# Keys and values of a second batch moved into the last head of the first, output weighting moved to ScalarE and accumulating transfers

## The reference, cut to what matters

```
xn = layernorm(x)
x  = x + attention(xn) + experts14(xn)      # 8 causal heads of 128, one key/value head; each row to 1 of 14 experts
xn = layernorm(x)
x  = x + scan(xn) + experts8(xn)            # selective state scan, 16 states; each row to 2 of 8 experts
```

## Time and profile before

| | |
|---|---|
| median of three runs | 759.58 us |
| profiled execution, its own time | 764.21 us |
| its span in the trace | 762.4 us |
| TensorE matmul busy | 672.0 us (88%) |
| VectorE busy | 539.8 us (71%) |
| ScalarE busy | 410.7 us (54%) |
| GpSimd busy | 236.7 us (31%) |
| mean granted TensorE clock | 0.951 of full |

### The profile page before, as it was taken

The page is one execution under the profiler, slowest core; times in us unless marked ns, Lnnn a source line. Parts: engine busy times, 40 slices in busy tenths (PEclk is TensorE's granted clock), DMA queues, the critical chain, the costliest instruction groups (busy, mean ns, idle before and its releaser), DMA issues. The chain is left out here.

```text
span 762.4 us, 11200 instructions
## 1 busy us (share of the span) xinstructions
PE 672.0 (88%) x3434; PEld 467.7 (61%) x3446; DVE 539.8 (71%) x830; ACT 410.7 (54%) x825; POOL 236.7 (31%) x183
## 2 busy tenths in 40 slices
PE   3988999999998989888899999998679779888685
PEld 2856777677765984544566566565535779878332
DVE  6165444344422224439899999999999999999998
ACT  1145665555651545575766667665746556666220
POOL 0012202212200005100222432332012866788874
PEclk9999999999997899999999999999969899999688
DMA  8400000000055482012366867778782454554112
GB/s 294 156 4 12 8 8 7 14 10 8 8 170 166 140 294 56 18 36 89 91 149 165 202 177 195 180 176 211 196 212 72 139 171 125 160 162 119 31 44 81
DMA packets 59806, 86.79 MB, mean 114 GB/s; under 512 B 7505, under 2 KB 35922, under 8 KB 59762
## 3 DMA queue, kind: packets, MB, share of 16 engines
q1 hardware_dynamic: 41330, 57.89, 24.6%
q0 software_dynamic: 7680, 23.08, 14.1%
q10 hardware_dynamic: 10752, 5.24, 2.3%
HBM read 54.60 MB, written 14.81 MB: 91 GB/s over the span
## 5 line engine op out<-in xcount | busy, mean ns | idle before, releaser
L1578 DVE TENSOR_REDUCE nmax<-PS 128x1 f32<-128x128 f32 (+7 forms) x128 | 96.1, 751 | 109.0 <-PE PS L1015 108.7
L1043 PE MATMUL PS<-ROOM 128*128 128x512 f32 (+3 forms) x384 | 141.7, 488 | 0.7 <-ACT ROOM L682 0.7
L682 ACT COPY ROOM<-PS 128x512 f32<-128x512 f32 (+1 forms) x192 | 85.8, 483 | 91.9 <-PE PS L1027 91.0
L689 ACT ACTIVATE ROOM<-PS,nmax 128x128 f32<-128x128 f32 (+7 forms) x128 | 95.6, 747 | 47.7 <-DVE nmax L1578 45.6
L1027 PE MATMUL PS<-CST,ROOM 128*128 128x128 f32 x576 | 85.9, 277 | 7.0 <-ACT ROOM L682 7.0
L559 POOL DMA_DIRECT2D ROOM<-ROOM x32 | 28.4, 889 | 202.0 <-DVE ROOM L1662 202.0
L1027 PEld LDWEIGHTS PS<-CST,ROOM 128*128 128x128 f32 x576 | 64.6, 142 | 34.3 <-issue 24.5
L1043 PEld LDWEIGHTS PS<-ROOM 128*128 128x128 f32 x384 | 65.0, 191 | 29.8 <-issue 25.8
L1012 PE MATMUL PS<-LATER 128*128 128x512 f32 (+2 forms) x192 | 74.5, 498 | 7.0 <-ACT ROOM L689 3.9
L524 POOL DMA_INDIRECT rows_in<-XN,slot x48 | 66.6, 1388 | 27.7 <-DVE slot L1491 14.4
L1654 DVE TENSOR_TENSOR_SCAN ROOM<-ROOM 128x1024 f32<-128x1024 f32 x32 | 72.8, 2275 | 0.9 <-ACT ROOM L725 0.2
(11 more groups left out here) (178 smaller groups left out, 1238.3 us busy)
## 6 DMA issues: line engine op xcount, KB each, us to landing
ROOM<-bc_rows SPq DMA_DIRECT2D x32, 512.0 KB, 4.3
ROOM<-ROOM POOLq DMA_DIRECT2D x32, 512.0 KB, 6.2
LATER<-in_w SPq DMA_DIRECT2D x48, 256.0 KB, 2.8
ROOM<-in_w SPq DMA_DIRECT2D x32, 321.0 KB, 3.8
rows_in<-zero SPq DMA_DIRECT2D x20, 256.0 KB, 3.3
LATER<-rows_in SPq DMA_DIRECT2D x24, 128.0 KB, 2.5
rows_out<-ROOM ACTq DMA_DIRECT2D x24, 128.0 KB, 2.2
ROOM<-rows_in SPq DMA_DIRECT2D x8, 256.0 KB, 4.2
```

The costliest lines, as they stand in the source:

```text
L682: nc.scalar.copy(dst, src).then_inc(s_ed, 1)
L689: nc.scalar.activation(PR[:, s, 0:nk], sc[:, 0:nk], ACT.Exp, bias=nmax[:, i % 4:i % 4 + 1], accum_out=rsum[:, i:i + 1]).then_inc(s_ex, 1)
L1043: r = mm(PS[:, 6, lo:BANK], V[:, j, :], PT[:, 4 * group + j, lo:BANK], start=j == 0, stop=True, skip_group_check=True)
L1578: nc.vector.tensor_reduce(nmax[:, i % 4:i % 4 + 1], sc[:, 0:(i + 1) * P], AX_X, ALU.max, negate=True).then_inc(s_nm, 1)
```

## The change

It has these parts.

1. TensorE's `keys_values(1)` is split into `keys(1)`, issued in `head_end` of head 7 between its last `turn` and its last `out_part`s, and `values(1)`, issued after these and ahead of the two projections. Their PSUM banks change to 0, 1 (keys) and 2, 3 (values). VectorE does its part of the keys between `inverse(7, 1)` and the two `add_out`. Before the experts TensorE now waits until the keys have left PSUM, and the first hidden product waits for the values' copies.
2. In batch 1 the identity product of the query becomes two fp32r products, of the identity with a high part PEH and with a low part PEL of pe. ScalarE makes PEH (one copy of 128x1024) ahead of the experts, after all scatters of the first expert layer; VectorE makes PEL (one subtraction) inside the experts. VectorE also copies the identity once at the start.
3. For heads 9 to 14 the weighting of the projection leaves VectorE. ScalarE's `weigh_out` writes bank 7 times the inverse row sum into a buffer OW (four instructions for each half), at tiles i = 3 and 7 of the next head, and GpSimd's `x_add` adds the half to x with an accumulating transfer. The additions of heads 8 and 15 stay on VectorE; head 15's wait for the transfers.
4. `combine_first(1)` moves from behind head 15 to the end of head 9.

```diff
@@ GpSimd
+            def x_add(g, s):
+                pool.wait_ge(s_we, 2 * g + 1 + s)
+                if g >= FIRST:
+                    pool.wait_ge(s_xo[s], 16 * (g - FIRST + 1))
+                else:
+                    pool.wait_ge(s_gu, NT)
+                nc.gpsimd.dma_start(X[:, TB + 4 * s:TB + 4 * s + 4, :], OW[:, 4 * s:4 * s + 4, :], accum_op=ALU.add
+                                    ).then_inc(s_xo[s], 16)
...
                     y_add(n, 1)
+                    x_add(FIRST + h - 1, 0)
...
                     y_add(n + 1, 1)
+                    x_add(FIRST + h - 1, 1)
@@ ScalarE
+            def weigh_out(g, s):
+                act.wait_ge(s_wo, 2 * g + 1 + s)
+                act.wait_ge(s_ri, 2 * g + 1 + s)
+                if g >= FIRST:
+                    act.wait_ge(s_xo[s], 16 * (g - FIRST + 1))
+                for t in range(4):
+                    r = nc.scalar.activation(OW[:, 4 * s + t, :], PS[:, 7, t * P:(t + 1) * P], ACT.Copy,
+                                             scale=rinv[:, 4 * s + t:4 * s + t + 1])
+                r.then_inc(s_we, 1)
...
+                    if pending and not split and i in (3, 7):
+                        weigh_out(g - 1, i // 4)
...
             keys_values(1)
+            act.wait_ge(s_sc[0], 16 * NT)
+            nc.scalar.copy(PEH[:], peT).then_inc(s_peh, 1)
@@ TensorE
                 if b:
-                    r = mm(bank(7), ident, peT[:, hf * BANK:(hf + 1) * BANK], start=False, stop=True)
+                    if isinstance(g, int) and g == HEADS:
+                        pe.wait_ge(s_pel, 1)
+                    mm(bank(7), identr[:], PEH[:, hf * BANK:(hf + 1) * BANK], start=False, stop=False)
+                    r = mm(bank(7), identr[:], PEL[:, hf * BANK:(hf + 1) * BANK], start=False, stop=True)
...
                 turn(g, 7)
+                if turned:
+                    turned()
                 for part in range(4):
                     out_part(g, b, 1, part)
...
-                head_end(g, b, 7)
+                head_end(g, b, 7, *((None, None) if b else (lambda: values(1), lambda: keys(1))))
...
-            keys_values(1)
+            pe.wait_ge(s_kf, 6)
             experts_first()
@@ VectorE
-                    if i == 3 and pending:
+                    if i == 3 and pending and not batch[0]:
                         add_out(g - 1, 0, x_prev)
...
-                    7: (lambda: first_drive(0, 0),)})
+                    7: (lambda: first_drive(0, 0), lambda: combine_first(1))})
...
-                head_end(7)
+                head_end(7, lambda: keys_values(1))
...
             dve.wait_ge(s_we, 32)
-            combine_first(1)
```

More of the change, by code:

```diff
@@ L84, in sem @@
             return ctx.enter_context(nc.semaphore(name))
+        with ExitStack() as second_half_of_XN:
+            second_half_of_XN.enter_context(nc.sbuf_tensor("under_PEH", [P, 3 * T], F32))
+            PEH = second_half_of_XN.enter_context(nc.sbuf_tensor("PEH", [P, T], F32R))
         X = sb("X", [P, NT, D])
@@ L136, in build @@
         HEAD_END, MOE_END, END = 53 * KB, 90 * KB, 133 * KB
+        identr = sb("identr", [P, P], F32R)
+        with ExitStack() as first_split:
+            PEL = first_split.enter_context(nc.sbuf_tensor("PEL", [P, T], F32R))
+            first_split.enter_context(nc.sbuf_tensor("under_KH", [P, END - T], F32))
+            KH, KL, QH, QL = (first_split.enter_context(nc.sbuf_tensor(n, [P, T], F32R)) for n in ("KH", "KL", "QH", "QL"))
         ROOM = sb("ROOM", [P, END])
-        with ExitStack() as first_split:
-            KH, KL, QH, QL = (first_split.enter_context(nc.sbuf_tensor(n, [P, T], F32R)) for n in ("KH", "KL", "QH", "QL"))
         LATER = sb("LATER", [P, 4 * T])
@@ L261, in build @@
         s_we = sem("projected_added")
+        s_xo = [sem(f"weighted_output_added{s}") for s in range(2)]
+        s_peh = sem("positions_high_ready")
+        s_pel = sem("positions_low_ready")
         s_mw = [sem(f"expert_weights{i}") for i in range(4)]
@@ L961, in _, with keys, values @@
             pe.wait_ge(s_cst, 16)
-            def keys_values(b):
-                quads = (2 * b, 2 * b + 1)
+            def keys(b):
                 pe.wait_ge(s_xnt, 2 * b + 2)
-                for q in quads:
+                for q in (2 * b, 2 * b + 1):
                     mm(bank(KEY_BANK[q]), wkv[:, 0:D], XNT[:, q * BANK:(q + 1) * BANK], start=True, stop=True).then_inc(s_kp, 1)
-                for q in quads:
-                    if q == 3:
-                        pe.wait_ge(s_kf, 5)
+            def values(b):
+                for q in (2 * b, 2 * b + 1):
                     for t in range(4):
@@ L978, in _ @@
             pe.wait_ge(s_cnv, 1)
-            keys_values(0)
+            keys(0)
+            values(0)
             transposes(1)
@@ L1108, in head, with head_end @@
                         out_part(g, b, 0, i - 6, not opening)
-            def head_end(g, b, h, between=None):
+            def head_end(g, b, h, between=None, turned=None):
                 turn(g, 6)
@@ L1535, in _ @@
             cp(identb[:], ident)
+            cp(identr[:], ident)
             cp(causalb[:], cst["causal"])
@@ L1561, in keys_values, with positions_low @@
                     tt(KL[:, sl], QF, KH[:, sl].bitcast(F32), ALU.subtract).then_inc(s_ke, 1)
+            def positions_low():
+                dve.wait_ge(s_peh, 1)
+                tt(PEL[:], peT, PEH[:].bitcast(F32), ALU.subtract).then_inc(s_pel, 1)
             keys_values(0)
@@ L1592, in add_out @@
                     dve.wait_ge(s_we, 2 * g + s - 1)
+                if batch[0] and g >= FIRST:
+                    dve.wait_ge(s_xo[s], 16 * (16 - FIRST))
                 for t in range(4):
@@ L1613, in head @@
                         q_evac(g + 1, 0)
-                    if i == 7 and pending:
+                    if i == 7 and pending and not batch[0]:
                         add_out(g - 1, 1, x_prev)
```

15 lines of the change are left out of this document (10 added, 5 removed).

## The result

The changed kernel takes 750.66 us (median of 13 runs, 748.77 to 756.37), the kernel before 759.58 beside it (13 runs): ratio 0.9898, 95% interval 0.9872 to 0.9924. The forecast was 751.7. The profiled execution took 751.28 us, its span is 749.4 us, the mean granted clock 0.957.

The account below looks back on a forecast made before the run. It took VectorE and TensorE as balanced in heads 10 to 15 and weight loads as setting the experts' end. Terms +1.0 - 1.2 - 5.5 - 2.2 = -7.9 us, from 759.58, gave 751.7 us; range 745 to 757.

Parts of the forecast that it names:

- What bounds the kernel: Heads 10 to 15: VectorE (25.4 us a head) and TensorE (25.7) in balance; relieving one alone gains almost nothing.
- Heads 10 to 15: Fewer identity products on TensorE, additions off VectorE: TensorE becomes the bound at 24.9 us a head, -5.5 us.
- the better bound of -6.7: Heads 10 to 15: the gain if all of TensorE's remaining waits for ScalarE go too (4.0 + 2.7 us).
- Gathered rows: Eight instructions move from behind head 15 to a VectorE wait at head 9's end: -2.2 us (-2.2 to 0).
- Head 8: The query's identity product as two fp32r products, where other engines wait for TensorE: -1.2 us (0 to -1.2).
- The seam: Between attention and experts: keys and values move into head 7, weight loads set the experts' end: +1.0 us.
- half-clock case: Seam: the clock falls after half of the values, the experts begin at 247.1 us and end 1.0 us later.
- the 3 us named as a sign against me: In the trace after, no VectorE wait on an accumulating transfer was to exceed 3 us.
- (c): Heads' accumulating transfers of x and y share one queue, products with C wait in twelve half heads: +17, 768.7 us; chance 0.07.
- (a): Seam: the clock holds through the values, -3.6 in place of +1.0, 747.1 us; chance 0.20.
- (b): Heads 10 to 15: ScalarE late or fp32r products no cheaper, 2 instead of 5.5 us gained, 755.2 us; chance 0.18.
- (d): Behind head 15 VectorE waits for transfers: the 2.2 us and a third of the 5.5 go, 755.7 us; chance 0.10.

Follow-up runs that it names:

- fp32_identity: The changed kernel with the query's identity product as one fp32 product again (part 2 undone in the products): 757.53 us, 0.997 of the kernel before.
- before_again: The kernel before, run again unedited: 758.68 us, 1.0009 of the kernel before.
- no_seam: The changed kernel with keys and values of the second batch again behind head 7 (part 1 undone): 750.55 us, 0.9892 of the kernel before.
- after_again: The changed kernel, run again unedited on the third chip: 751.68 us, 0.9899 of the kernel before.
- gather_late: The changed kernel with batch 1's gathered rows added behind head 15 again (part 4 undone): 754.1 us, 0.9935 of the kernel before.
- vector_adds: The changed kernel with the weighted additions of heads 9 to 14 on VectorE again (part 3 undone): 757.8 us, 0.9996 of the kernel before.

## Why the prediction was right, step by step

**What bounds the kernel.** Right in that both engines had to be relieved for the whole gain: 1.5 and 5.3 us alone, 8.0 together. But "work taken from one alone gains almost nothing" holds for TensorE only. VectorE's relief alone gave 0.78 us in each of heads 11 to 14 and 1.9 in head 15, two thirds of the whole. The needs as I had them allowed 0.5 us a head (26.16 to TensorE's 25.7); but a part of that 25.7 was waits for ScalarE, which end when the maxima come earlier. The whole times say it less clearly. Without the products' part 0.3% of the 1.0% is left, without the additions' part 0.0%, neither to be told from zero, but the first of these kernels also had a long seam and a wait behind head 15.

**Heads 10 to 15: -5.5 forecast, -8.0 measured,** and the better bound of -6.7 was passed. This term was mis-sized at two places. The step took TensorE as the bound in every head. In head 15 it makes one half query, not two, as no head follows; from head 14's wide maximum to head 15's pass 25.4 us before and 23.3 after (485.80 to 509.14): 2.1, nearly all of VectorE's 2.2, where I gave 0.9. Of these the additions alone give 1.9 and the products alone nothing, so VectorE is the bound there. In heads 11 to 14 the period fell from 26.20 to 24.79. Of these 1.41 us the products are 2 x 0.39 = 0.78, and the waits for ScalarE about 0.45, which all went where I gave a bit over half; some 0.2 us a head I can't place. ScalarE's cost was right: 13.6 us for 13.8, 127.3 busy for 126, and hidden.

**Gathered rows: -2.2,** measured -2.1, and undone +2.2. **Head 8: -1.2,** measured -1.2.

**The seam: +1.0 by the half-clock case.** The mechanism came as told, at other minutes: the clock fell after 21 records or so, not 16, so the projections began at 238.79 for 240.3, the experts at 245.38 for 247.1, quad 4's weights went at 256.16 for 257.8. The rule that loads set the end held: head 8's query begins 29.2 to 30.9 us behind quad 4's issue in thirteen of the fourteen traces, and 31.4 in fp32_identity, with issues from 244.22 to 257.23. What failed is that I took the seam of one execution as the kernel's. Over three traces of the old order (before, before_again, no_seam) it is 65.7 us (63.5 to 67.7), over five of the new one (after, after_again, gather_late, fp32_identity, vector_adds) 66.6 (65.3 to 68.8): +0.9 on average. That this is near the forecast's +1.0 is luck: with this spread only "no large gain" is shown, as no_seam's time says too.

**Profiles and medians.** The later stages give -1.2 - 8.0 - 2.1 = -11.3 between the traces, the medians 8.9. Between them lie the seam's +0.9 and what the wait behind head 15's scatters adds to the way, 0.7 us on the mean of eleven traces; some 0.8 us are open. I had that wait as 0, at most +3, and in after_again and no_seam it was 3.34 and 3.50, over the 3 us named as a sign against me. It is a late transfer, as rival (c) has it, but in one half head of twelve. So the forecast of 751.7 came within 1.1 us of 750.66 partly by luck: the heads gave 2.5 us more than I counted, and the wait and the open 0.8 us took most of it back. The first trace of before was also 7.2 us longer than the second, all but 0.3 of it ahead of head 8's query.

**The rivals.** (a) is out for this kernel: the clock fell in every trace with the values in one piece and their bias products. Its price was of the right size: I gave 4.6 us, and the split that holds the clock gives 4.0, by one pair of traces. (b) is out: 13.6 us of weighting were hidden and the products cost 0.39 less. (c) is out as a rule of every half head, though not by my argument: an `x_add` has half the bytes and yet lands later after its issue than a `y_add`, 8.4 us for 6.6. A `y_add` doesn't stand behind it for that long; its own median rose by 0.4 us only. (d) is out: from the statistics to the end it is 224.2 us as against 224.6.

The Trainium skill ("TensorE: Matmul & The Clock Gate", "HAM oscillation — how this bites in real kernels") ties the loss of the clock to long idle gaps. Here it fell inside 128x128 products that alternate with one-row ones, with the engine busy throughout as the profile draws it: in after without a wait from 223.5 to the fall at 235.5. In before it had also fallen at 234.2, behind two waits of 1.22 us, and come back at 237.6, before the fall at 241.0. The measurement decides against idle gaps as the only cause. What it is in these products isn't shown. Without the one-row products, or with eight dense projection products between two halves, the clock didn't fall there, but then no stretch of value products was longer than 3.3 us. That the experts' 128x128 products, 172 records in 21 us, kept 1.00 speaks for the one-row ones as the cause.

## What to carry to other kernels

Where two engines are nearly in balance, judge parts that relieve one each alone and together, and by the period of a stage rather than the whole time: 1.5 and 5.3 us alone were 8.0 together. Before explaining a stage by two traces, take a second trace of the same program and see how far that stage moves by itself. Moving work ahead gains nothing if what it moves past releases the loads that set the end. Freeing these loads alone shortened the seam by 0.8 us, with TensorE's wait for the last addition moved too by 4.6, and with dense products between the two halves of the narrow ones by 4.0 more; each is read from one or two traces, in a stage that moves by 3 to 4 us by itself. Check a granted clock of 1.00 against the steps of the products.

## What the runs showed of the hardware

- 32 alternating products (128x128, one-row) take 0.21 us each at 2.4 GHz and 0.36 at 1.2 GHz; the 16 without the one-row ones 0.11 each at 2.4 GHz. The granted clock fell to half 3 to 6 us into the first kind in all eleven traces with them in one piece in batch 1, without a gap among them.
- Accumulating transfers of 256 KB, each issued right behind one of 512 KB, land 7.8 to 8.6 us after issue (medians of eleven traces, 8.4 in after), those of 512 KB after 5.6 to 7.0 (6.6 in after; 6.2 to 6.4 in the three traces without the smaller ones). They take 1.2 and 0.9 us of GpSimd's time.
- The head 7 wide maximum comes at 216.8 to 217.0 us in seven traces and at 219.4 to 219.9 in seven. In the second seven the values of batch 0 step at the pace of 1.2 GHz from their second pair on, with 1.00 shown as the clock; in the first seven most of the first half steps at full pace. What decides between the two is open.
- In all four profiles of one chip the way from head 8's query to its wide maximum took 9 to 11 us longer than elsewhere, with TensorE, VectorE and ScalarE standing and GpSimd working on (VectorE's longest wait there is 8.3 to 11.8 us), and the kernel before was 1.4% slower on it. What stopped them is open.
